# Transformer block on one core: where the masked softmax weights are spread over the partitions, and which engine makes which low parts of x

## The reference, cut to what matters

```
xn   = layernorm(x)                            # x is [8, 512, 1024], float32
q, k, v = split(xn @ w_qkv.T + b_qkv)          # 8 heads of 64
scores[f, t] = k[f] . q[t], or -10000 where f > t
attn = softmax over f                          # vals[t] = sum_f attn[f, t] v[f]
x = x + layernorm(vals @ w_o.T + b_o)
x = x + layernorm(x' @ W.T + b + routed low-rank product),  x' = layernorm(x)
```

## Time and profile before

| | |
|---|---|
| median of 3 runs | 1557.02 us (1556.56 to 1557.93) |
| the profiled execution | 1556.95 us, its span 1555.1 us |
| attention phase | up to about 899.6 us of the span |
| one batch in the loop | 107.2 us, the same in all seven to 0.02 us |
| last batch of the attention phase | about 107.9 us |
| output phase | about 655 us |

### The profile page before, as it was taken

One profiled execution on the slowest core, in us unless ns is written; L12 is line 12 of the kernel. 1 busy time (PEld: TensorE's weight loads), 2 busy tenths in 40 slices (PEclk: granted clock), 3 DMA queues, 4 the chain that ended last, 5 costly groups with the idle time before them and its releaser, 6 DMA issues. The chain is left out here.

```text
span 1555.1 us, 25025 instructions
## 1 busy us (share of the span) xinstructions
PE 1493.2 (96%) x8032; PEld 1308.3 (84%) x8032; DVE 981.6 (63%) x2112; ACT 696.7 (45%) x1499; POOL 611.5 (39%) x1156
## 2 busy tenths in 40 slices
PE   6999999999999999999999779999999999999996
PEld 5878878878878888788888569999999999999996
DVE  7475575664765755756646656666666666666663
ACT  5364464563663644645635643333333333333331
POOL 2352452442442523524422534444434443344433
PEclk9999999999999999999999889999999999999998
DMA  6212112112112121031111712211122211111211
GB/s 241 74 38 83 43 29 89 34 52 63 44 48 71 37 75 53 24 94 34 51 24 38 237 58 68 68 67 67 67 67 67 67 63 62 57 65 57 67 62 41
DMA packets 46927, 102.93 MB, mean 66 GB/s; under 512 B 5040, under 2 KB 21424, under 8 KB 46896
## 3 DMA queue, kind: packets, MB, share of 16 engines
q1 hardware_dynamic: 46896, 102.54, 21.2%
HBM read 60.06 MB, written 25.69 MB: 55 GB/s over the span
## 5 line engine op out<-in xcount | busy, mean ns | idle before, releaser
L1466 PE MATMUL ps_f<-wagh,x2Th 128*128 128x364 f32 x768 | 256.4, 334 | 4.4 <-DVE f L1328 2.9
L1466 PE MATMUL ps_f<-wagl,x2Th 128*128 128x364 f32 x768 | 253.6, 330 | 0.0
L1466 PE MATMUL ps_f<-wagh,x2Tl 128*128 128x364 f32 x768 | 253.2, 330 | 0.0
L923 PE MATMUL ps_o<-xTh,wh 128*128 128x512 f32 x504 | 203.4, 404 | 8.8 <-DVE xTl L551 6.7
L923 PE MATMUL ps_o<-xTh,wl 128*128 128x512 f32 x504 | 198.0, 393 | 0.0
L923 PE MATMUL ps_o<-xTl,wh 128*128 128x512 f32 x504 | 197.1, 391 | 0.0
L1466 PEld LDWEIGHTS ps_f<-wagh,x2Th 128*128 128x128 f32 x768 | 145.5, 189 | 7.2 <-issue 5.0
L1466 PEld LDWEIGHTS ps_f<-wagl,x2Th 128*128 128x128 f32 x768 | 145.6, 190 | 1.3
L1466 PEld LDWEIGHTS ps_f<-wagh,x2Tl 128*128 128x128 f32 x768 | 145.4, 189 | 0.0
L1199 POOL TENSOR_TENSOR var_eps<-mv,eps 128x1 f32<-128x1 f32 x95 | 19.1, 201 | 300.0 <-DVE mv L1262 300.0
L447 POOL TENSOR_SCALAR pr<-pr,rden 128x128 f32<-128x128 f32 (+3 forms) x256 | 136.6, 552 | 0.0
(11 more groups left out here) (172 smaller groups left out, 3565.5 us busy)
## 6 DMA issues: line engine op xcount, KB each, us to landing
kst<-kst SPq DMA_DIRECT2D x64, 256.0 KB, 3.6
xt<-in_x SPq DMA_DIRECT2D x32, 512.0 KB, 4.0
out<-outs SPq DMA_DIRECT2D x32, 512.0 KB, 3.1
xs<-in_x SPq DMA_DIRECT2D x24, 512.0 KB, 4.5
valsT<-vt SPq DMA_DIRECT2D x64, 128.0 KB, 2.3
vraw<-valsT SPq DMA_DIRECT2D x32, 256.0 KB, 4.2
raw<-in_wqkvT SPq DMA_DIRECT2D x12, 512.0 KB, 5.6
wag_raw<-in_wagT SPq DMA_DIRECT2D x8, 546.0 KB, 5.8
```

The source lines that it names most:

```text
L923: done = pe.matmul(ps[:, :], w[:, k, c:c + P], xT[:, k, :], start=(k == 0 and w is wh and xT is xTh), stop=(k == KD - 1 and w is wl), skip ...
L1466: last = pe.matmul(ps_f[:, g, 0:GW], a[:, k, :], w[:, k, cols], start=(k == 0 and a is x2Th and w is wagh), stop=False, skip_group_check=True)
```

## The change

- The masked weights are spread by three matmuls of 128 columns (`masked_weights`). The stationary operand is one column of wn, repeated 128 times by a step of zero; the moving operand is the identity in float32r (identr, made once). Dw, its instruction on POOL, the ones matrix and the semaphore d_ready go.
- They stand in the next slot's first projection part, behind its first two k steps, and wait for wn and for DVE's low part of the previous head's second group. So they come ahead of the slot's transposes and not after them.
- ACT's copy to WT moves from the end of its slot to the head of it, ahead of the exponentials. WT has two rooms, by head.
- The second group of transposes waits for that copy, and `values` no longer waits for it.
- Low parts of x: POOL now has row tiles 0 and 1 of g = 0 and row tiles 2, 3 and 1 of g = 1; DVE has 2 and 3 of g = 0 and 0 of g = 1.
- The reload of the late part of wl on SP waits for the projection ("k", 0) of the next batch and not for POOL's low parts.

```diff
-        WT = sb("WT", [P, 3 * P], F32R)
-        Dw = sb("Dw", [P, 3 * P], F32R)
-        ones = sb("ones", [P, P], F32R)
+        WT = sb("WT", [P, 2, 3 * P], F32R)
+        identr = sb("identr", [P, P], F32R)
...
-        wn = sb("wn", [P, 2, 4], F32)
+        wn = sb("wn", [P, 2, 4], F32R)
...                                     (SP)
-                        sp.wait_ge(x_lo_pool, 4 * b + 8)
+                        sp.wait_ge(k_full, 4 * b + 5)
...                                     (POOL)
-                pool.wait_ge(wn_done, H + 1)
-                if h > 0:
-                    pool.wait_ge(wt_ready, H)
-                pool.tensor_tensor(Dw[:, :].rearrange("p (i t) -> p i t", i=3),
-                                   ident[:, :].unsqueeze(1).to_broadcast([P, 3, P]),
-                                   wn[:, q, 0:3].unsqueeze(2).to_broadcast([P, 3, P]), ALU.mult).then_inc(d_ready, 1)
...
-                for t in (2, 3):
-                    if g == 0:
-                        pool.wait_ge(x_hi_act, 6 * b + t - 5)
+                for t in ((0, 1) if g == 0 else (2, 3, 1)):
+                    if g == 0 or t == 1:
+                        pool.wait_ge(x_hi_act, 6 * b + 4 * g + t - 5)
...                                     (DVE, x_low)
-                for t in range(2):
+                for t in ((2, 3) if g == 0 else (0,)):
...                                     (ACT)
             def masked_spread(h, b):
-                act.wait_ge(t_full[1], 2 * (8 * b + h) + 2)
-                act.activation(WT[:, :], ps_t[1][:, 0:3 * P], ACT.Copy).then_inc(wt_ready, 1)
+                act.wait_ge(t_full[1], 2 * (8 * b + h) + 1)
+                act.activation(WT[:, h % 2, :], ps_t[1][:, 0:3 * P], ACT.Copy).then_inc(wt_ready, 1)
...
                     late = h == BEHIND or last and h >= BARE
+                    if 1 <= h <= NH:
+                        masked_spread(h - 1, b)
...
                         p_hi(h - 1, 2, b)
-                        masked_spread(h - 1, b)
...                                     (PE, project)
-                        pe.wait_ge(x_lo_dve, 8 + 4 * b - 2 + k // 2)
-                        pe.wait_ge(x_lo_pool, 4 + 4 * b - 2 + k // 2)
+                        pe.wait_ge(x_lo_dve, 8 + 3 * b - (1 if k == 0 else 0))
+                        pe.wait_ge(x_lo_pool, 5 * b - (3 if k == 0 else 0))
...
+            def masked_weights(h, b):
+                H = 8 * b + h
+                pe.wait_ge(wn_done, H + 1)
+                if h > 0:
+                    pe.wait_ge(t_lo, 3 * H - 1)
+                for i in range(3):
+                    last = pe.matmul(ps_t[1][:, i * P:(i + 1) * P], wn[:, h % 2, i:i + 1].to_broadcast([P, P]),
+                                     identr[:, :], start=True, stop=True)
+                last.then_inc(t_full[1], 1)
...                                     (PE, transpose_p; for g == 1)
-                    pe.wait_ge(wt_ready, H)
+                    pe.wait_ge(wt_ready, H + 1)
...
-                if g == 3:
-                    pe.wait_ge(d_ready, H + 1)
-                    pe.matmul(ps_t[bank][:, 0:3 * P], ones[:, :], Dw[:, :], start=True, stop=True)\
-                        .then_inc(t_full[bank], 1)
-                    return
...                                     (PE, values)
-                pe.wait_ge(wt_ready, H + 1)
...                                     (PE, steps)
+                    if n == 0 and part == 0 and 1 <= h <= NH:
+                        step(kind, p, row, ks[:2], last)
+                        masked_weights(h - 1, b)
+                        step(kind, p, row, ks[2:], last)
...
+                if part == 0 and 1 <= h <= NH and not between(h, part, b, last):
+                    masked_weights(h - 1, b)
...                                     (PE, body)
                         transpose_p(h - 1, 2, b)
-                        transpose_p(h - 1, 3, b)
```

More of the change, by code:

```diff
@@ L181, in attention_phase @@
         eps = sb("eps", [P, 1], F32)
-        hold = sb("hold", [1, 6], F32)
+        hold = sb("hold", [1, 5], F32)
         nm = sb("nm", [P, 2, 4], F32)
@@ L496, in _ @@
             pool.memset(hold[:, 0:1], 0.0).then_inc(held, 1)
-            pool.memset(hold[:, 3:4], 0.0).then_inc(x_lo_pool, 4)
-            pool.wait_ge(consts, 12)
+            pool.wait_ge(consts, 11)
             pool.affine_select(out=ident[:, :], in_=ident[:, :], compare_op=ALU.not_equal, fill=1.0, base=0,
@@ L503, in _ @@
                                pattern=[[-1, P]], channel_multiplier=1).then_inc(consts, 1)
+            pool.wait_ge(consts, 13)
+            pool.tensor_scalar(identr[:, :], ident[:, :], 1.0, 1.0, ALU.mult, ALU.mult).then_inc(consts, 1)
             for t in range(NT):
@@ L927, in project, with project_v @@
                     done.then_inc(k_full if kind == "k" else q_full, 1)
-                elif (kind, p) == ("q", 3) and not last:
+                elif KD // 2 - 1 in ks and (kind, p) == ("q", 3) and not last:
                     done.then_inc(x_read, 1)
-            def project_v(t, b):
-                if t == 0:
+            def project_v(t, b, ks):
+                if 0 not in ks:
+                    pass
+                elif t == 0:
                     pe.wait_ge(wl_back, 16 * b + 16)
@@ L938, in project_v @@
                     pe.wait_ge(v_low, 4 * b + t - 1)
-                for k in range(KD):
+                for k in ks:
                     w_high = wh[:, k, 2 * PART:3 * PART]
@@ L943, in project_v @@
                                          start=(k == 0 and xT is xTh and w is w_high), stop=(k == KD - 1 and xT is xTl))
-                done.then_inc(v_full, 1)
+                if KD - 1 in ks:
+                    done.then_inc(v_full, 1)
             def scores(h, b):
@@ L1003, in values @@
                     if j > 0:
-                        last = pe.matmul(ps_v[:, 0:j * P], v[:, j, h, :], WT[:, 0:j * P],
+                        last = pe.matmul(ps_v[:, 0:j * P], v[:, j, h, :], WT[:, h % 2, 0:j * P],
                                          start=False, stop=(j == NT - 1), skip_group_check=True)
@@ L1016, in first_output, with step @@
                 done.then_inc(first_out, 1)
-            def steps(h, part, b, last):
-                for kind, p, row, ks in between(h, part, b, last):
-                    if kind == "v":
-                        project_v(p, row)
-                    else:
-                        project(kind, p, row, ks, last)
+            def step(kind, p, row, ks, last):
+                if kind == "v":
+                    project_v(p, row, ks)
+                else:
+                    project(kind, p, row, ks, last)
+            def steps(h, part, b, last):
+                for n, (kind, p, row, ks) in enumerate(between(h, part, b, last)):
+                    if n == 0 and part == 0 and 1 <= h <= NH:
+                        step(kind, p, row, ks[:2], last)
+                        masked_weights(h - 1, b)
+                        step(kind, p, row, ks[2:], last)
+                    else:
+                        step(kind, p, row, ks, last)
+                if part == 0 and 1 <= h <= NH and not between(h, part, b, last):
+                    masked_weights(h - 1, b)
             def turns(h, place, b, last):
```

22 lines of the change are left out of this document (10 added, 12 removed).

## The result

The median went from 1557.95 us (1555.04 to 1559.62, 20 runs) to 1554.40 us (1552.37 to 1556.40, 20 runs). The ratio is 0.9978, with a 95% interval of 0.9971 to 0.9985: 3.55 us less, 0.22% faster. The forecast was 6.1 us less, 1550.9 us.

The account below looks back on a forecast made before the run. PE, busy 96% of the span, bounds the kernel. Terms sum to -0.86 us a batch, times seven -6.0, and -0.1 in the last: -6.1, forecast 1550.9 us; range 1544 to 1558.5, likeliest 1547 to 1554 (0.57).

Parts of the forecast that it names:

- slots 2 and 3: In each loop batch, slot 2 pays the full 0.35 us and slot 3 saves 0.65.
- the cover in slot 5: Slot 5: PE's waits for x and at L986 cover the 0.35 us of the three new matmuls.
- the collision: Slot 5: DVE's three-column L604 may miss POOL's L470; nothing to half of 1.09 us, taken as 0.2.
- Three matmuls at 0.35 us: On PE, three 128-column matmuls cost 0.12 us each, 0.35 together; net +0.18 per slot where PE never waits.
- cheaper at 0.17: Rival: weight loads hide, three matmuls cost 0.17 us, the kernel takes 1544.4 us; chance 0.15.
- dearer from 0.50: Rival: repeated column loads slowly, three cost 0.81 us, total time 1572 us; outweighs the gain from 0.50; chance 0.11.
- The wait of L980 goes: Ends of slots 3, 5 and 7: L980's 0.46 us wait for PTl disappears; transposes to projection shrinks by 0.65.
- Slots 4 and 5: In each loop batch, slot 4 pays +0.18 us and slot 5 saves 0.80, between 0.6 and 1.1.
- ACT's copy at the head of its slot: ACT's copy, waiting for PE until 1.7 us into the slot, is covered by idle time ahead of the exponentials.
- the sign I had named: Prediction is wrong if ACT's exponentials start later relative to the scores than before in slots 3, 5 or 7.
- that rival: ACT's copy delays the chains of slots 3, 5, 7 by 0.35 us each; 7.3 us back, 1558.2; chance 0.17.
- The last batch at -0.1: Last batch: slots 1, 2, 4 cost 0.71 us, slot 3 gives 0.65, slot 8 saves 0.17; together -0.1.

Follow-up runs that it names:

- the kernel with the earlier transposes: The changed kernel with the transposes of x (2, 0) moved amid an earlier projection of slot 3, DVE's statistics for them to slot 2; 1550.83 us.
- The kernel with POOL's wait: The kernel before with only the new shares of x, plus POOL's second tile of x waiting for nm; 1547.85 us against 1557.72, ratio 0.9937.
- its copy: The kernel named just ahead of it, profiled once more without an edit: the change 1557.0 us, the kernel before 1560.21 us.
- the old form: The changed kernel with one 384-column matmul of POOL-made diagonal blocks at the new place, behind three k steps, in the loop's seven batches; 1550.27 us.
- all parts: The changed kernel with one 384-column matmul at the new place, earlier transposes of x and POOL's wait for nm; 1548.59 us against 1557.72, ratio 0.994.

## Why the prediction was half right

The forecast was 6.1 us less, and 3.55 were measured; 1554.40 us lies just above the 1547 to 1554 that had the best chance. Two terms were wrong against the change, slots 2 and 3 and the cover in slot 5, and one was wrong in its favour, the collision. That they partly made up for each other is luck.

**Three matmuls at 0.35 us, right.** 0.33 measured in slot 1, 0.33 more for three more, and +0.74 a batch at the old place. This rules out both rivals on the price: cheaper at 0.17 and dearer from 0.50. What I had put down to "a weight load that so short a matmul does not cover" fits the one matmul of 384 columns, with one load, at 0.17; no run tests the load by itself.

**Slots 1, 4 and 8 at +0.18, about right.** Slot 1 gave +0.11, slot 4 +0.25, slots 8 and 9 +0.29.

**Slots 6 and 7, right.** -0.32 for -0.30, and the wait for the second PTl is gone.

**Slots 2 and 3, wrong, and this is the step that failed.** It stands under "The wait of L980 goes": "In slots 3, 5 and 7 L980 waited [...] so 0.65 is saved". I had read slot 3 as "alike" slot 7, but PE's last work before the transposes there is the transposing of x into a bank that the slot's next projection writes. Before, ACT's copy out of it was hidden behind L980's wait; with that gone the copy is what is late next, 0.67 us from transposes to projection in place of 0.22. The rows of slot 3 were on the table, with PE alone; ACT's row of the kernel before, beside them, would have shown it:

```profile
302.91 0.60 ACT L720 ACTIVATE xs<-ps_o 128x512 f32<-128x512 f32 x1 [0.51 <-PE ps_o L888]
```

The copy ends at 303.51, and L980 stood at 303.54. PE's wait of 0.37 us ahead of the transposes was no cover either: the copy follows PE's transposes of x, so the new matmuls push it back by their full price. Slots 2 and 3 gave +0.23 where -0.30 was forecast. The size is settled by the kernel with the earlier transposes, which took 0.48 us off slot 3 and 0.50 off the batch, seven times that 3.5 us. The loop missed its forecast by less, 1.6 us, because slots 4 and 5 gained 0.3 a batch more than forecast.

**Slots 4 and 5, low in size, by two errors.** DVE's shorter job gave 0.59 for 0.6. For the collision of nm with POOL I had taken 0.2 as a guess between nothing and 0.5. The exponentials had waited 0.92 us for nm, and no longer do. And "0.35 is covered" was wrong for slot 5: with nm out of the way the exponentials wait for ACT's high parts of x, which wait for PE, and start 0.35 us later with the new matmuls than without. So slot 5 gained 0.59 + 0.92 - 0.35 = 1.16 (1.18 measured), and the group 0.93 for 0.62. I saw the collision, and left it as a small term with a guess. The kernel with POOL's wait shows the largest gain of any single edit here: 0.86 us a batch.

**ACT's copy at the head of its slot, covered as forecast.** Behind their scores the exponentials start as before in slots 3 (6.90 us) and 7 (5.28), and earlier in slot 5 (6.77, before 7.34), so the sign I had named did not show. The wait did come back through ACT, by other instructions than that rival named: in slot 3 by the copy of x, and in slot 5 by the high parts of x, where the comparison with before hides it.

**The last batch at -0.1, off by 1.1 us, not settled.** With the masked weights at the old place it took 106.67 to 108.27 us in four executions (before, its copy, shares of x alone, the same with POOL's wait), and 108.93 with three matmuls there. At the new place it took 108.00 to 108.82 in four (the change, its copy, masked weights alone, earlier transposes), and 106.50 and 109.96 in the old form and in all parts, whose last batch is the change's but for one k step more ahead of the new matmuls. The clock is part of the scatter: of the last two, PE ran at 1.2 GHz for 6.8 us in the first and 23.4 in the second; but the time does not follow it closely, 108.45 with 20.1 us beside 108.82 with 13.7. Up to a microsecond may be the change's, in the empty slots 6 to 8, where I had let the chain hide everything. No run separates that from the scatter.

## What to carry to other kernels

Before a wait is removed, list what all engines do at that place, and name the second latest releaser: places that look alike in the bounding engine's row can have different ones. A tiny instruction that takes several times its normal duration is no noise; look for what runs beside it, and try one wait that holds the other engine back for it before rearranging work. If a change is two edits, run each alone: here one half was worth nothing by itself, and the other met a collision that the first had moved. And a stage that came out shorter does not show that the new work in it was covered; here a larger gain hid its price.

## What the runs showed of the hardware

- DVE's operation on 128x3 values in SBUF took 0.17 us with POOL idle, and 0.38, 1.09 and 1.30 us with a POOL operation of 128x512 under way (0.52 and 0.28 beside Dw, of 128x384). By the records one by one, it ended 0.025 us behind POOL's tile each time: 321.092 and 321.067 in the change, 322.283 and 322.258 before, 322.482 and 322.457 with the shares of x alone. In the last it had come 0.01 us after the tile began and waited for all of it. The Trainium skill (SBUF — State Buffer, section "SBUF: two separate sides") says that DVE and GpSimd share one port pair, and that an instruction that gets it keeps it to its end, while an instruction of the other engine that needs it is blocked. The trace agrees for this operation. It was not so for every one: DVE's four maxima of slot 5, which read PSUM, took 1.68 us with POOL's tile beside them in the shares of x alone, and 1.68 in slot 2 before, where POOL was all but idle.
- Matmuls in float32r with a stationary operand of one repeated column are issued every 0.10 us (six in 0.61 us), plus 0.05 behind the last, at the granted clock of 1.00. Their weight loads took 188 ns, as those of the projections did. For matmuls of 128 columns with their loads the Trainium skill (TensorE: Matmul & The Clock Gate, section "Back-to-back issue gap") has 81 ns as the sustained spacing. The runs show more, and the measurement decides.
- The stretches outside the loop scatter where the loop does not. The start up to the first batch took 40.4 to 43.3 us in 14 profiled executions, with PE at 1.2 GHz for none, 3.4 or 6.8 us of it, and the output phase 655.2 to 657.9. The loop's batches agree to 0.1 us between two executions of the same kernel. So effects of some tenths of a microsecond are read from the loop's trace, and not from one execution's total.
